# A fused transformer block on one core: first loads by row tiles and units, key tiles summed on GpSimd, a second place for split x1 forms

## What is computed

```python
# x: (4, 512, 1024); wq, wo: (1024, 1024); wk, wv: (1024, 256)
q, k, v = x @ wq, x @ wk, x @ wv          # split into heads of 32
q, k = rope(q), rope(k)
attn = softmax(causal(q @ k.T / sqrt(32)))
x = layernorm(x + (attn @ v) @ wo)
# gate_t, up_t: (3584, 1024), down_t: (1024, 3584), values -1, 0, 1
hidden = silu(x @ (gate_t * gate_s).T) * (x @ (up_t * up_s).T)
x = layernorm(x + hidden @ (down_t * down_s).T)
```

## Time and profile before

| | us |
|---|---|
| median of 3 runs | 1943.39 |
| lowest and highest | 1939.68, 1946.0 |
| the profiled execution, its own time | 1941.53 |
| its span, first to last instruction | 1939.8 |
| PE busy | 1831.0 (94%) |
| DVE busy | 1147.3 (59%) |
| ACT busy | 774.9 (40%) |
| POOL busy | 491.9 (25%) |

### The profile page before, as it was taken

One profiled execution on the slowest core, in us unless ns is written; L12 is line 12 of the kernel. 1 busy time (PEld: TensorE's weight loads), 2 busy tenths in 40 slices (PEclk: granted clock), 3 DMA queues, 4 the chain that ended last, 5 costly groups with the idle time before them and its releaser, 6 DMA issues.

```text
span 1939.8 us, 27794 instructions
## 1 busy us (share of the span) xinstructions
PE 1831.0 (94%) x10592; PEld 890.5 (46%) x10592; DVE 1147.3 (59%) x2028; ACT 774.9 (40%) x1166; POOL 491.9 (25%) x999
## 2 busy tenths in 40 slices
PE   3999999999999987888999999999999999999997
PEld 1654654555555633333444444444444444444443
DVE  5787777677767754446444454665644544446645
ACT  4254444344434433345343343342343433334421
POOL 0164546455536556221000000211300000001204
PEclk8999999999999999998999999999999999999999
DMA  7524234443324395736131231448532213214201
GB/s 242 130 51 93 51 83 113 91 81 103 95 50 117 82 223 156 230 107 230 55 109 66 87 99 67 138 143 157 187 101 87 89 67 105 77 55 152 87 12 76
DMA packets 228020, 210.61 MB, mean 109 GB/s; under 512 B 183856, under 2 KB 184112, under 8 KB 227888
## 3 DMA queue, kind: packets, MB, share of 16 engines
q1 hardware_dynamic: 227024, 208.45, 37.5%
q10 hardware_dynamic: 864, 0.39, 0.1%
...
## 4 chain that ended last, share of the span: by engine, by line
PE 84%; DMA 5%; DVE 3%; SPq 2%; ACT 2%; issue 2%; POOL 1%; ACTq 0%; DVEq 0%; POOLq 0%
PE bank L840 33%; PE bank L855 20%; PE bank L746 17%; PE bank L794 4%; PE bank L758 3%; PE bank L782 3%; PE bank L805 2%; SPq L1325 2%; PE bank L761 1%; DMA x_forms_spill<-x_parts 1%; DMA w_page<-gateT 1%; DMA page<-wo 1%; DMA page<-xT 0%; DVE row_max L1024 0%; DMA page<-wq 0%
## 5 line engine op out<-in xcount | busy, mean ns | idle before, releaser
L840 PE MATMUL bank<-x_forms,weight_forms 128*128 128x512 f16 x3136 | 717.2, 382 | 32.4 <-DVE gate_blocks L1124 9.2
L840 PEld LDWEIGHTS bank<-x_forms,weight_forms 128*128 128x128 f16 x3136 | 306.6, 98 | 414.8 <-issue 18.8
L855 PE MATMUL bank<-w_down,hid 128*128 128x512 f16 x1792 | 413.2, 379 | 2.4 <-DVE hid L1141 2.4
L906 ACT ACTIVATE p_tiles<-bank 128x512 f32<-128x512 f32 (+1 forms) x352 | 192.8, 556 | 299.3 <-PE bank L782 297.1
L855 PEld LDWEIGHTS bank<-w_down,hid 128*128 128x128 f16 x1792 | 175.3, 98 | 214.1 <-DVE hid L1141 2.9
L1024 DVE TENSOR_REDUCE row_max<-bank 128x1 f32<-128x384 f32 (+3 forms) x352 | 219.7, 636 | 90.6 <-PE bank L761 89.7
L1229 POOL TENSOR_TENSOR acc<-acc,down_scale 128x1024 f32<-128x1024 f32 x16 | 38.6, 2410 | 779.0 <-DVE acc L1162 779.0
L746 PE MATMUL bank<-wq_parts,xT_parts 128*128 128x256 f16 x1536 | 217.8, 274 | 12.9 <-DVE wq_parts L988 12.7
L746 PE MATMUL bank<-wo_parts,att_parts 128*128 128x512 f16 x768 | 194.3, 381 | 10.4 <-DMA att_parts<-att_spill 10.4
L1195 POOL TENSOR_SCALAR_AFFINE_SELECT p_tiles<-p_tiles 128x128 f32<-128x128 f32 (+2 forms) x352 | 137.4, 398 | 227.2 <-ACT p_tiles L906 226.2
L746 PEld LDWEIGHTS bank<-wq_parts,xT_parts 128*128 128x128 f16 x1536 | 142.9, 98 | 59.9 <-DVE wq_parts L988 15.6
...
## 6 DMA issues: line engine op xcount, KB each, us to landing
w_page<-gateT SPq DMA_DIRECT2D x56, 512.0 KB, 4.4
w_page<-upT SPq DMA_DIRECT2D x56, 512.0 KB, 4.5
w_page<-downT SPq DMA_DIRECT2D x56, 512.0 KB, 4.6
...
att_parts<-att_spill SPq DMA_DIRECT2D x16, 512.0 KB, 3.5
x_row<-x_spill SPq DMA_DIRECT2D x16, 512.0 KB, 3.3
out<-acc SPq DMA_DIRECT2D x16, 512.0 KB, 2.7
```

What stands on the lines that cost most here:

```text
L840: t = nc.tensor.matmul(strassen[bank_set(use)][to][:, :], w_form[:, use % 4, A_FORMS[a_form], k * P:(k + 1) * P], xF[:, :, B_FORMS[b_form] ...
L855: t = nc.tensor.matmul(to[:, :], hid[g % 2][:, c, a, i % 2, i // 2 * P:(i // 2 + 1) * P], w_down[:, g % 2 * GC + c, cols], start=g == grou ...
L906: nc.scalar.activation(p32[j][:, h0:h0 + heads, :], bank[5 + m % 2][:, 0:heads * n].rearrange("p (h c) -> p h c", c=n), ACT.Exp, scale=SCO ...
```

## The change

- **Page contents.** A page of x holds one row tile (128 rows, all eight chunks), one of wq holds half of the chunks for one unit's 256 columns; wkv and wo pages stay. `FIRST` gives an order of 12 first pages, and the remaining wq pages come later through `page0` and `page1`. A projection waits for its own row tile and its own unit's pages, and the x tile of the next batch may be split when the last unit has projected that tile.
- **Sums.** `presum` also adds tile 1 into tile 0, in two halves of two heads (two instructions of 768 elements a partition), and `sums` multiplies only tile 0 by ones. The `exp` of `j` = 1 to 3 waits for the `presum` that reads the tile, that of `j` = 0 for `sums`.
- **Buffers.** `x1_p` gets two places, each with a semaphore for its stores. `rope_sin` keeps one place instead of two, so `rotate` waits for the `rope_add` before it.
- **Order.** Tile 9 moves from slot 14 to slot 15. The scale bounds (`bound`) are made after unit 1's projections instead of first. The planner's DMAs take .4 us of the queue and then share one queue of moves.

In the diff, line numbers of the file before are not kept. "..." marks what is left out.

```diff
@@ plan and its constants @@
-OUT_SLOTS = (4, 5, 7, 8, 9, 11, 12, 13, 14, 14, 15, 15)
+OUT_SLOTS = (4, 5, 7, 8, 9, 11, 12, 13, 14, 15, 15, 15)
+PRE_PARTS = (2, 1, 1)
+PRE = [(j, n) for j in reversed(range(NT - 1)) for n in range(PRE_PARTS[j])]
+LANDS = 1.9
+PAGE_MOVES, FORM_MOVES, TURN_MOVES = 1.85, .95, 1.31
+FIRST = (("wkv", 0, 0), ("x", 0, 0), ("wkv", 0, 1), ("wkv", 0, 2), ("wkv", 0, 3), ("wq", 0, 0), ("wq", 0, 1),
+         ("x", 0, 1), ("x", 0, 2), ("x", 0, 3), ("wq", 1, 0), ("wq", 1, 1))
+NFIRST = len(FIRST)
...
+            if moves:
+                queue = max(queue, now + us) + moves
+                lands = queue + LANDS - free[e]
...
-    loads = [(w, 0, j) for j in range(KD // 2) for w in ("x", "wkv")] + [("wq", 0, k) for k in range(KD)]
-    ranks = {w: -100.0 + n for n, w in enumerate(loads)}
+    ranks = {w: -200.0 + n for n, w in enumerate(FIRST)}
+    for g in range(2, UNITS):
+        for half in range(2):
+            ranks["wq", g, half] = SLOT * (g - 3) + 5 * half
     for b in range(1, B):
-        for j in range(KD // 2):
-            ranks["x", b, j] = SLOT * (UNITS * b - 2) - 3 + j
+        for t in range(NT):
+            ranks["x", b, t] = SLOT * (UNITS * b - 3 + (t + 1) / NT)
...
+            [("proj", "q", UNITS * b - 1, j, KD - 1)] if what == "x" and b else []))
...
-        put(VE, end, 1.0, "rotate", *one, after=[made] + ([("rotate", *one_back)] if r else []) + (
+        put(VE, end, 1.0, "rotate", *one, after=[made] + ([("rotate", *one_back), ("rope_add", *one_back)] if r else []) + (
...
-        freed = [("pv", *last, j), ("sums", *last) if j < 2 else ("presum", *last, j - 1)] if q else []
+        freed = [("pv", *last, j)] + ([("presum", *last, j - 1, n) for n in range(PRE_PARTS[j - 1])] if j else [("sums", *last)]) if q else []
...
-        if j in (1, 2):
-            put(PO, at + 4, .2 + REP * (S - (j + 1) * P) / 410, "presum", u, G, j,
-                after=[("pv", u, G, j)] + [("presum", u, G, 2)] * (j == 1))
+        for n in range(PRE_PARTS[j]) if j < NT - 1 else ():
+            before = ("presum", u, G, j, n - 1) if n else ("presum", u, G, j + 1, PRE_PARTS[j + 1] - 1) if j < NT - 2 else (
+                "presum", *last, 0, PRE_PARTS[0] - 1)
+            put(PO, at + 4, .2 + REP * (S - (j + 1) * P) / 410 / PRE_PARTS[j], "presum", u, G, j, n,
+                after=[("pv", u, G, j)] + ([before] if q or j < NT - 2 or n else []))
         if j:
-        put(PE, at + 3.5, 1.5, "sums", u, G, takes="T", after=[("causal", *one), ("presum", u, G, 1)])
+        put(PE, at + 7, .9, "sums", u, G, takes="T", after=[("presum", u, G, 0, PRE_PARTS[0] - 1)])
...
-    plan.put(VE, -300, .4, "bound", 0)
-    plan.put(PO, -300, 3.0, "bound", 0, 0, after=[("bound", 0)])
-    plan.put(VE, -299, .8, "bound", 1, after=[("bound", 0, 0)])
+    plan.put(VE, SLOT, .4, "bound", 0, after=[("proj", "q", 1, NT - 1, KD - 1)])
+    plan.put(PO, SLOT, 3.0, "bound", 0, 0, after=[("bound", 0)])
+    plan.put(VE, SLOT, .8, "bound", 1, after=[("bound", 0, 0)])
...
-        ropeB = sb(A, "rope_sin", [2, UH * HD], F32)
+        ropeB = sb(A, "rope_sin", [UH * HD], F32)
-        x1_p = sb(A, "x1_parts", [2, HALF], F16)
+        x1_p = sb(A, "x1_parts", [2, 2, HALF], F16)
...
+            if what == "x":
+                return [xT_p[:, a, :, j * P:(j + 1) * P] for a in range(2)]
+            if what == "wkv":
+                return [wkv_p[:, a, 2 * j:2 * j + 2, :] for a in range(2)]
+            if what == "wq":
+                return [wq_p[:, a, 4 * j:4 * j + 4, b * UH * HD:(b + 1) * UH * HD] for a in range(2)]
+            return [wo_p[:, a, j:j + 1, :] for a in range(2)]
...
-                    on.wait_ge(s_caus, key_n(u, G, 0, REP - 1) + 1)
-                    on.wait_ge(s_pre, 2 * (u * UG + G + 1))
+                    on.wait_ge(s_pre, len(PRE) * (u * UG + G + 1))
                     trans_free((kind, *which))
-                    for j in range(2):
-                        for h in range(REP):
-                            t = nc.tensor.matmul(bank[TRANS][h * HD:(h + 1) * HD, j * P:S], ones[:, :], p32[j][:, h, :],
-                                                 start=j == 0, stop=j == 1, tile_position=(0, h * HD))
+                    for h in range(REP):
+                        t = nc.tensor.matmul(bank[TRANS][h * HD:(h + 1) * HD, :], ones[:, :], p32[0][:, h, :],
+                                             start=True, stop=True, tile_position=(0, h * HD))
...
-                        on.wait_ge(s_proj, proj_n["q", which[1] * UNITS - 1, NT - 1] + 1)
-                    nc.scalar.activation(parts_of(*which)[0], src, ACT.Copy,
+                        on.wait_ge(s_proj, proj_n["q", which[1] * UNITS - 1, which[2]] + 1)
+                    nc.scalar.activation(parts_of(*which)[0], as_parts(which[0], src), ACT.Copy,
...
-                    if j < 2:
+                    if j == 0:
                         on.wait_ge(s_sums, q)
-                    else:
-                        on.wait_ge(s_pre, 2 * q - (j - 2))
+                    elif q:
+                        on.wait_ge(s_pre, len(PRE) * (q - 1) + PRE.index((j - 1, PRE_PARTS[j - 1] - 1)) + 1)
...
-                    on.wait_ge(s_xF, 16 * made_n[which])
-                    nc.scalar.activation(x1_p[:, 0, :], x1_form_of(*which), ACT.Copy, scale=X1_UP).then_inc(s_x1hi, 1)
+                    n = made_n[which]
+                    on.wait_ge(s_xF[n % 2], 16 * (n // 2))
+                    nc.scalar.activation(x1_p[:, n % 2, 0, :], x1_form_of(*which), ACT.Copy, scale=X1_UP).then_inc(s_x1hi, 1)
...
-                    on.wait_ge(s_add, r - 1)
+                    on.wait_ge(s_add, r)
...
-                    u, G, j = which
+                    u, G, j, n = which
                     q = u * UG + G
+                    heads = slice(n * REP // PRE_PARTS[j], (n + 1) * REP // PRE_PARTS[j])
                     on.wait_ge(s_pv, NT * q + NT - j)
-                    on.wait_ge(s_pre, 2 * q + 2 - j)
-                    to = p32[j][:, :, P:S - j * P]
-                    nc.gpsimd.tensor_tensor(to, to, p32[j + 1][:, :, :], ALU.add).then_inc(s_pre, 1)
+                    on.wait_ge(s_pre, len(PRE) * q + PRE.index((j, n)))
+                    to = p32[j][:, heads, P:S - j * P]
+                    nc.gpsimd.tensor_tensor(to, to, p32[j + 1][:, heads, :], ALU.add).then_inc(s_pre, 1)
                 elif kind == "newton":
...
-        "xT": x.reshape(B, S, KD, P).transpose(0, 3, 2, 1),
+        "xT": x.reshape(B, NT, P, KD, P).transpose(0, 1, 4, 3, 2),
-        "wq": chunked(heads_split(g["attn_wq"], NH)),
+        "wq": heads_split(g["attn_wq"], NH).reshape(2, KD // 2, P, UNITS, UH * HD).transpose(3, 0, 2, 1, 4),
```

117 lines of the change are left out of this document (59 added, 58 removed).

## The result

| | before | after |
|---|---|---|
| median of 4 runs, us | 1943.28 | 1930.59 |
| lowest to highest, us | 1939.68 to 1946.00 | 1929.70 to 1931.62 |
| profiled execution, span, us | 1939.8 | 1929.9 |
| busy PE, DVE, ACT, POOL, us | 1831.0, 1147.3, 774.9, 491.9 | 1817.4, 1172.8, 766.8, 617.5 |

The ratio is 0.9936, with a 95% interval of 0.9919 to 0.9953: 12.7 us faster, where 39 were forecast. The direction was right; 1930.6 lies above the range's end of 1926.

The account below looks back on a forecast made before the run. TensorE was taken to set the pace in attention, with its idle time counting elsewhere. Terms -11 + 1 - 20.7 + 7 - 6 - 10 = -39.7 us took 1941.5 to 1901.8; with 1.9 for the median, 1904 us, range 1883 to 1926.

Parts of the forecast that it names:

- opening, with maxima: Kernel start: second key/value projection begins at 34.5 us instead of 45.4, -11 us; less cover for the maxima's DMA, +1 us.
- `bound` moved: Behind unit 1, in attention: free DVE time hides its few short instructions, no cost; about 3 us once without cover.
- matmuls of the sums: Attention: 32 groups lose four matmuls of 384 columns on TensorE, -20.7 us, bounds -19 to -21.
- new waits: Attention: sums and others wait for GpSimd's two halves where cover is short, +7 us, bounds 0 and +32.
- batch changes: Attention at batch changes: row tiles let the first x tile be split three projections earlier, -6 us, bounds 0 and -9.6.
- end of attention: 693 to 920 us: third out tile in slot 15 and two places for x1 forms, together -10 us, bounds 0 and -22.
- the slow start of tile 0's matmuls: Opening: tile 0's 24 matmuls run at the half clock first and take 9 to 10 us.
- the line of the sums: Sign in the profile after: the sums' source line at 33 us, where both forms cost 54.1 us before.
- The rule of the shared port: Attention: two-input DVE and GpSimd instructions reading SBUF exclude each other; DVE at most 41 of 45 us, not the pace.
- The rival built on it (1929 us): GpSimd late in every group: sums or exp of tile 1 about 1 us late in all 32; 1929 us, chance 0.15.
- the 4 us for out tiles: End of attention, slot 15: a third out tile takes 4 of TensorE's 11.2 us idle time.
- the 6 for the second place of x1: End of attention: two places take most of ScalarE's 37.2 us store wait away, saving 6 of TensorE's 17 us idle.

Follow-up runs that it names:

- b1s2: Kernel after the change, with the bound back in the opening and the row sums over two key tiles as before: 1917.80 us, ratio 0.9865.
- b1: Kernel after the change, with only the bound of the softmax scales worked out in the opening again: 1922.53 us, ratio 0.9893.
- b1o1: Against b1s2, same order, the four 384-column matmuls a group not issued and no added GpSimd work (key tile 1 missing from divisor): 1901.07 us, ratio 0.9792.
- s2: Kernel after the change, with the row sums over two key tiles on TensorE as before and no halves on GpSimd: 1926.19 us, ratio 0.9914.
- o1: Against s2, same order, the four 384-column matmuls a group not issued and no added GpSimd work (key tile 1 missing from divisor): 1907.16 us, ratio 0.9804.
- p0: Kernel after the change, order and waits kept, GpSimd's add of key tile 1 cut to one column per head: 1928.62 us, ratio 0.9920.
- slots: Against b1s2, the last out tiles at slots 14, 14, 15, 15 as before the change: 1917.99 us.
- x1one: Against b1s2, one place instead of two for the split forms of x1: 1915.61 us.

## Why the prediction was wrong, step by step

| step | forecast, us | measured, us |
|---|---|---|
| opening, with maxima | -11 + 1 | -12.3 after, -10.4 in `b1s2`, in the account at 95 us |
| `bound` moved | 0 | +8.1 (`b1`) |
| matmuls of the sums | -20.7 | -16.7 and -19.0 (`b1s2` to `b1o1`, `s2` to `o1`) |
| new waits | +7 (0 to +32) | +21.5 for order, waits and GpSimd's work together (`b1` less `b1o1`) |
| batch changes | -6 | no gain seen: 95 to 693 us lost 4.8 more than before in `b1s2` |
| end of attention | -10 (0 to -22) | -22.2 in `b1s2`, -10.6 after |

- **The opening** came nearly as worked out: the first matmul and the place of the transpose in the queue were right, and the second key/value projection began 14.7 us sooner instead of 11, of which 12.3 were left at 95 us. The granted clock was 0.50 (1.2 GHz) again from 30 to 36 us, behind 3.8 us without TensorE's work. I had put the slow start of tile 0's matmuls down to the half clock; in the windows of that stretch the granted clock reads 1.00 (12 to 22 us after), though up to 16 us they ran near the pace of the 0.50 stretch, twelve in 3.8 us against six in 2.
- **`bound`** is the first step that failed: a cost that I put at nothing, and it was 8 us. I said that DVE's free time "hides" it and that without cover it "would cost about 3 us once", and read that price off instructions. In the rows of before it stood between 10.3 and 13.1 us, where GpSimd had nothing else to do, so what lies around it could not be seen. I gave it no range either. An estimate by the section of the Trainium skill named above, "GPSIMD Engine Reference", "Instruction dispatch", would have been about 6 us.
- **The new waits** are the second step that failed and the largest miss, some 14 us: the term charged the halves' uncovered time alone, and what the runs show instead is 21.5 us for the order made to cover it and the waits that this order brings, of which cutting the halves to a column gives back 2 at most. The duration (1.85 us forecast, 1.89 measured) and the line of the sums (33 forecast, 35.0 measured) were right. I counted the cover in the new order and charged only the groups that lack it. But the cover is not free: it is TensorE's other work brought forward or held back, and what it covered before is then bare. That shows where I did not look, as the waits for `row_max` and `causal` in the table above, and in the last unit. `sums` itself waits little, 8.9 us, 6.9 of them behind the all-reduce. Of the 21.5 us some 9 go with the two new dependences; the rest was not taken apart.
- **The rule of the shared port**: the mean `nat_lo` rose from 532 to 799 ns, so the trace agrees with the section "Who interferes with whom" of the Trainium skill's "SBUF — State Buffer"; with the halves cut to a column (`p0`) it is 629, and without them (`b1s2`) 584. But DVE was not the pace, and `p0` gained 2 us. The rival built on it (1929 us) gave nearly the measured time for a reason that the runs don't bear out.
- **Batch changes** show no gain: in the three windows of the earlier trace rows that hold one TensorE was busy for 128.45 us before and is for 126.69 after. No run undoes the row-tile pages of x, or the one place of `rope_sin`, by itself, so why the 6 us did not come stays open.
- **The end of attention**: the 4 us for out tiles and the 6 for the second place of x1 were both wrong (`slots`, `x1one`), so -10.6 against my -10 was luck. Of the -22.2 in `b1s2`, 18 came from a line of the diff to which I gave no term, the planner's account of the queue, and the kernel after lost 11.6 of the 22.2 again, 9.1 of them with the sums (in that stretch `b1` loses 44.9 us and `b1s2` 35.8). In `b1s2` the terms of the opening, batches and end add up to the forecast's -26, but by two errors against each other.

The parts as measured: -26.4 (all but bound and sums) + 4.7 + 8.1 = -13.6 us. This is the chain of medians 1944.2, 1917.8, 1922.5, 1930.6 and checks nothing by itself; the 0.9 us to the measured -12.7 are the difference between two medians of the kernel before.

**A version that beats both:** `f1s2`, 1914.99 us, ratio 0.9840 to before: the change without its sums, with `bound` back in the opening, and the opening's queue mended.
